# Expert stage of a decoder layer: the down product's two remainder matmuls, widened with zeros before, one in each row half of the array after

## The reference, cut to what matters

```
E, I, TOPK = 64, 192, 8
CAP = 2 * (M * TOPK) // E            # 256 token places per expert
...
h = silu(einsum('ecd,edi->eci', xe, gate_proj)) * einsum('ecd,edi->eci', xe, up_proj)
ye = einsum('eci,eid->ecd', h, down_proj)
out = zeros((m, d)).at[tok].add(contrib)   # contrib: the rows of ye, weighted
x = x + out
```

## Time and profile before

| | us |
|---|---|
| median of three runs | 1675.92 |
| lowest and highest of them | 1671.69 to 1676.97 |
| span of the profiled execution, first to last instruction | 1678.1 |
| expert stage in it, from the first transfer of its POOL program on | about 542 |

### The profile page before, as it was taken

How to read it: one execution, slowest core, us unless ns; L and a number is a source line. 1 busy time by engine, 2 the same in 40 slices (tenths; PEclk the granted TensorE clock), 3 DMA queues, 4 the chain that set the end, 5 groups by cost and what they waited for, 6 DMA issues and landing times. The chain is left out here.

```text
span 1678.1 us, 28691 instructions
## 1 busy us (share of the span) xinstructions
PE 1419.7 (85%) x9603; PEld 1053.1 (63%) x9603; DVE 1050.1 (63%) x2044; ACT 972.8 (58%) x1969; POOL 759.6 (45%) x492
## 2 busy tenths in 40 slices
PE   2889889899986767898898887856999999999990
PEld 2677777677764533444444433336999999999980
DVE  4666666667663533434443449855888888888880
ACT  3555455455552335674574575625777777777770
POOL 2344344444431013633533430003777777777762
PEclk9989999999997989998998998877999999999995
DMA  8000000000002276475466266055999999999986
GB/s 323 1 14 26 14 14 26 14 25 15 20 8 88 70 135 115 88 121 143 75 110 158 51 115 115 4 166 174 288 298 297 299 297 294 294 296 293 296 170 125
DMA packets 133106, 229.79 MB, mean 137 GB/s; under 512 B 17865, under 2 KB 51145, under 8 KB 132496
## 3 DMA queue, kind: packets, MB, share of 16 engines
q1 hardware_dynamic: 103184, 154.98, 34.0%
q0 software_dynamic: 29248, 72.53, 19.5%
q10 hardware_dynamic: 576, 0.98, 0.2%
HBM read 163.78 MB, written 71.83 MB: 140 GB/s over the span
## 5 line engine op out<-in xcount | busy, mean ns | idle before, releaser
L1045 ACT ACTIVATE shared<-xa_ring 128x1024 f32<-128x1024 f32 x256 | 247.0, 1030 | 94.1 <-PE xa_ring L1445 93.9
L1007 POOL TENSOR_TENSOR shared<-shared,xa_half 128x32 f32<-128x32 f32 x24 | 130.3, 5429 | 248.0 <-DVE shared L1168 248.0
L302 POOL TENSOR_TENSOR sa_prob<-sa_prob,sa_rinv 128x1024 f32<-128x1024 f32 x64 | 121.3, 1896 | 244.7 <-DVE sa_rinv L465 244.7
L1612 POOL DMA_INDIRECT ex_xg<-xn,token x128 | 173.9, 1359 | 82.2 <-issue 57.6
L360 ACT ACTIVATE sa_prob<-sa_sc_ps,sa_nmax 128x256 f32<-128x256 f32 x256 | 118.0, 473 | 111.1 <-DVE sa_nmax L452 111.1
L95 PE MATMUL ex_ba<-ex_xh,ex_wh 128*128 128x256 f32 x512 | 149.6, 292 | 4.4 <-DVE ex_xl L1726 3.7
L97 PE MATMUL ex_ba<-ex_xh,ex_wl 128*128 128x256 f32 x512 | 145.7, 285 | 0.0
L96 PE MATMUL ex_ba<-ex_xl,ex_wh 128*128 128x256 f32 x512 | 145.6, 284 | 0.0
L1457 PE MATMUL xa_out<-shared 128*17 128x512 f32 x1024 | 140.3, 621 | 0.5 <-ACT shared L1045 0.4
L1713 DVE TENSOR_TENSOR ex_wl<-shared,ex_wh 128x1024 fp32r<-128x1024 f32 (+1 forms) x128 | 116.9, 955 | 36.1 <-ACT ex_wh L1656 36.1
L452 DVE TENSOR_REDUCE sa_nmax<-sa_sc_ps 128x2 f32<-128x512 f32 x128 | 83.1, 687 | 66.5 <-PE sa_sc_ps L597 66.5
(11 more groups left out here) (223 smaller groups left out, 3939.7 us busy)
## 6 DMA issues: line engine op xcount, KB each, us to landing
shared<-in_L_ffn_gate_proj_dram SPq DMA_DIRECT2D x64, 384.0 KB, 5.7
shared<-in_L_ffn_up_proj_dram SPq DMA_DIRECT2D x64, 384.0 KB, 7.3
turned<-stage SPq DMA_DIRECT2D x64, 256.0 KB, 2.8
shared<-in_L_ffn_down_proj_dram SPq DMA_DIRECT2D x64, 256.0 KB, 5.0
xa_kT<-turned SPq DMA_DIRECT2D x96, 128.0 KB, 8.3
xa_qT<-turned SPq DMA_DIRECT2D x96, 128.0 KB, 10.5
shared<-in_L_ffn_down_proj_dram SPq DMA_DIRECT2D x64, 128.0 KB, 6.3
sa_x<-in_x_dram SPq DMA_DIRECT2D x16, 256.0 KB, 2.8
```

The costliest lines, as they stand in the source:

```text
L302: pool.tensor_tensor(prob[:, 4 * g:4 * g + 4, :], prob[:, 4 * g:4 * g + 4, :], rinv[:, 4 * g:4 * g + 4].unsqueeze(2).to_broadcast([P, 4, 2 ...
L1007: pool.tensor_tensor(power[:, i], ms[:, i], half[:], ALU.pow).then_inc(s_pw, 1)
L1045: act.activation(prob[:, w % 2, 2 * i:2 * i + 2, :], ring[i][:], ACT.Exp, scale=D2 ** -0.5).then_inc(s_ex[i], 1)
L1612: pool.indirect_dma_start(out=xg[:, e % RING, j, :], out_offset=None, in_=xn3, in_offset=bass.IndirectOffsetOnAxis(token[:, at:at + 1], 0))\
```

## The change

The low by high product of the remainder takes 64 rows of the array for each token tile in place of 128. Token tile 0 keeps its low part of h in rows 0 to 63 and is multiplied by `dh[0:64, i, 1]`; token tile 1 has its low part of h in rows 64 to 127 and is multiplied by a new tile `dr`, a copy of the same high part of the down matrix in rows 64 to 127. The two matmuls stand side by side at the end of `down`, after the four others of both token tiles. For that ACT makes one more copy for each expert, from partitions 0 to 63 to partitions 64 to 127; DVE makes `hl` of the remainder in two pieces of 128 columns in place of one of 256, the second one into partitions 64 to 127; and nothing is set to zero any more. PE and SP wait for the new copy.

```diff
--- before.py
+++ after.py
@@ -1535,6 +1535,7 @@
         wl = m.sb("wl", [P, 2, C, 3, P], F32R)
         dh = m.sb("dh", [P, 2, 2, D], F32R)
         dl = m.sb("dl", [P, 2, D], F32R)
+        dr = m.sb("dr", [P, 2, D], F32R)
         xg = m.sb("xg", [P, RING, CT, XW])
         xh = m.sb("xh", [P, 2, C, CAP], F32R)
         xl = m.sb("xl", [P, 2, C, CAP], F32R)
@@ -1550,7 +1551,7 @@
 
         ld_g = [m.sem(f"ld_g{k}") for k in range(RING)]
         st_y = [m.sem(f"st_y{k}") for k in range(RING)]
-        st_out, s_zero = m.sem("st_out"), m.sem("zero")
+        st_out = m.sem("st_out")
         counters = []
 
         def counter(name):
@@ -1597,6 +1598,7 @@
                     wait(sp, s_wl, 2 * e + 2)
                     weights_of.load_gate_up(sp, e + RING, k)
                     wait(sp, s_dl, DL * e + DL)
+                    wait(sp, s_dh, 3 * e + 3)
                     weights_of.load_down(sp, e + RING, k)
 
             loop(sp, lambda: None, step, lambda: None)
@@ -1625,7 +1627,6 @@
                                             oob_is_err=False, compute_op=ALU.add)\
                         .then_inc(st_y[e % RING], 16)
 
-            pool.memset(hl[R:2 * R, :, 1].bitcast(F32), 0.0).then_inc(s_zero, 1)
             gather(0)
             gather(1)
             for e in range(E):
@@ -1660,6 +1661,7 @@
                 wait(act, s_dn, 2 * e - 2)
                 act.activation(dh[:, i, 0], rawd[:, k, 0], ACT.Copy).then_inc(s_dh, 1)
                 act.activation(dh[0:R, i, 1], rawd[0:R, k, 1], ACT.Copy).then_inc(s_dh, 1)
+                act.activation(dr[R:2 * R, i], rawd[0:R, k, 1], ACT.Copy).then_inc(s_dh, 1)
 
             def tokens(e, i):
                 for j in range(CT):
@@ -1713,9 +1715,9 @@
                     dve.tensor_tensor(lo, src, hi.bitcast(F32), ALU.subtract).then_inc(s_wl, 1)
 
             def down_weights(e, i, k):
-                dve.wait_ge(s_dh, START + 2 * e + 1)
+                dve.wait_ge(s_dh, START + 3 * e + 1)
                 dve.tensor_tensor(dl[:, i], rawd[:, k, 0], dh[:, i, 0].bitcast(F32), ALU.subtract).then_inc(s_dl, 1)
-                dve.wait_ge(s_dh, START + 2 * e + 2)
+                dve.wait_ge(s_dh, START + 3 * e + 2)
                 dve.tensor_tensor(dh[R:2 * R, i, 1], rawd[0:R, k, 1], dh[0:R, i, 1].bitcast(F32),
                                   ALU.subtract).then_inc(s_dl, 1)
 
@@ -1733,7 +1735,10 @@
             def inner_low(e, i):
                 dve.wait_ge(s_hh, START + 3 * e + 2)
                 dve.tensor_tensor(hl[:, i, 0], h[:, i, 0], hh[:, i, 0].bitcast(F32), ALU.subtract).then_inc(s_hl, 1)
-                dve.tensor_tensor(hl[0:R, i, 1], h[0:R, i, 1], hh[0:R, i, 1].bitcast(F32), ALU.subtract).then_inc(s_hl, 1)
+                for j in range(CT):
+                    at = slice(j * P, (j + 1) * P)
+                    dve.tensor_tensor(hl[j * R:(j + 1) * R, i, 1, at], h[0:R, i, 1, at], hh[0:R, i, 1, at].bitcast(F32),
+                                      ALU.subtract).then_inc(s_hl, 1)
 
             def store(e, k, r):
                 dve.wait_ge(s_dn, START + 2 * e + 2)
@@ -1784,7 +1789,8 @@
             def down(e, i):
                 pe.wait_ge(s_dl, START + 2 * e + 2)
                 pe.wait_ge(s_hh, START + 3 * e + 3)
-                pe.wait_ge(s_hl, START + 2 * e + 2)
+                pe.wait_ge(s_hl, START + 3 * e + 3)
+                pe.wait_ge(s_dh, START + 3 * e + 3)
                 for j in range(CT):
                     wait(pe, (s_yA, s_yD)[j], e)
                     at = slice(j * P, (j + 1) * P)
@@ -1792,10 +1798,12 @@
                             lambda c: dl[:, i], 1, stop=False)
 
                     pe.matmul(by[j][:], hh[:, i, 1, at], dh[:, i, 1], start=False, stop=False)
-                    pe.matmul(by[j][:], hl[:, i, 1, at], dh[:, i, 1], start=False, stop=True).then_inc(s_dn, 1)
+
+                for j, rest in enumerate((dh[0:R, i, 1], dr[R:2 * R, i])):
+                    pe.matmul(by[j][:], hl[j * R:(j + 1) * R, i, 1, j * P:(j + 1) * P], rest, start=False,
+                              stop=True).then_inc(s_dn, 1)
 
             def first():
-                pe.wait_ge(s_zero, 1)
                 turn(0, 0, 0)
 
             def step(e, k, r):
```

## The result

The changed kernel takes 1698.99 us (median of 4 runs, 1696.4 to 1706.46) against 1673.81 us for the kernel before (median of 4, one run more than in the table above): 1.0154 times as long, 95% interval 1.0124 to 1.0185. That is some 25 us slower; forecast were 16, between 4.6 and 22.6, so the result lies above the range.

What follows compares the result with a forecast made beforehand. PE, waiting for `xl` in a loop through ACT and DVE, was taken as the bound. 61 x 0.29 = 17.7 us, less 1 for long experts and 0.5 at the start, gave +16 us: 1692 us, range 1680 to 1698.

Steps and rivals of the forecast that it cites:

- What bounds the kernel before: Per expert, a loop of `up` (PE), silu (ACT), h and `xl` (DVE) sets the period, 7.56 us; PE waits for `xl`.
- The copy on ACT: ACT's new copy `dr` ahead of the `wh` copies: 0.77 us against 0.48 slack, so h comes 0.29 us later per expert.
- The pair on PE: The two half matmuls ending `down`: 0.43 to 0.45 us with both switches, against 0.46 before; gains 0.01 to 0.03 us.
- The store on ACT now waits: Token tile 0's last matmul comes later in `down`, so ACT's store starts 0.26 us too late.
- the second loop: Store and copies on ACT, `wl` and h on DVE, `hh` copies, next store: 7.08 us, 7.85 with the new copy.
- The two-expert loop: From the late store through copies, `wl`, h, `xl`, `up` and down: 0.55 us longer, 0.27 to 0.28 per expert.
- The long experts: Experts that already took longer, 1.3 us in all, would mostly be taken in by a loop with slack on PE: -1 us.
- The two loops counted once: The second loop and the two-expert loop run side by side, so 0.29 us per expert was counted only once.
- DVE, POOL, the start: Split `hl` on DVE and POOL's work cost nothing; without zeros POOL's first gather starts earlier, -0.5 us or nothing.
- No change: Rival, about 1676 us: the loop over `up` stays the bound, the copy hides in ACT's 1.57 us wait; chance 0.10.
- faster: Rival, about 1661 us: PE is the bound, the pair takes one matmul's time, saving 0.23 us per expert; chance 0.04.
- slower still: Rival, above 1700 us: PE's switches cost say 0.3 us each, not 0.10, making the store 0.2 later; chance 0.06.

## Why the prediction was right in its direction and too small

**What bounds the kernel before.** Right. PE waits for `xl` by a hair: with the wait moved back the period fell to 7.48 us, 7.47 was expected of that run.

**The copy on ACT.** Right, in place and in size: 0.78 us for 0.77, a period of 7.86 for 7.85, and 0.53 for a copy that stays in its partitions, where 0.52 was put. The rows of L1678, a copy of another length, gave the price.

**The pair on PE.** Wrong. It was put at 0.43 to 0.45 us for 0.46, neutral. The switch in (0.32 for 0.33) was read rightly; the way back was taken from a switch to yet another small division, 0.33 us, and to the full array it is 0.42 to 0.43, with a first matmul of `up` that is 0.11 longer. The pair alone loses 0.16 us per expert. In the changed kernel the way back is hidden, since the other loops are longer: with the other order in `up` its period is 7.86 us, that of the copy, and not PE's 7.64.

**The store on ACT now waits.** Right as a mechanism, and here lies the missed size: "the same as the second loop within what I can read". The two-expert loop was put at 2 x 7.56 + 0.55 = 15.67 us and is 15.88 (7.85 + 8.03) or 16.12 (7.85 + 8.27). The step that failed is the size of one term, the way from the start of the pair to the store, put at 0.40 + 0.04 = 0.44 us ("ends 0.40 later", and ACT sees it 0.04 later). A half whose weights are not loaded ahead is listed with 0.50, and the earlier trace rows had it so. The store comes 0.53 us after the pair even in the written-out steps, and 0.64 in the hardware loop, with 0.11 of it for the scale's address, a term that the forecast did not have. That is 0.20 per two experts, 15.87 for the 15.88 measured, and 30 x 0.20 = 6 us.

**The long experts.** Wrong by sign: 1 us was taken off because a loop with slack on PE would take them in. The loop of the copy does, in the run with the copy alone. The two-expert loop runs through PE and does not: in the twelve long turns of it the loop takes 0.23 us more on average, 3 us in all. These and the 6 above are about what lies between 16 and 25.

**The two loops counted once.** Half right. The longer one counts, which is what was said; but it was the two-expert loop, at 7.99 us on average, and not 7.85. With 7.85 the sum gave 16 us, and the run with the copy alone, where only that loop is there, took 16.6 in its stage.

**DVE, POOL, the start.** The split `hl` costs no time: the run without the copy has it, and is PE's. From ACT's first copy of the stage (1135.55 before, 1127.01 after) to the first transposes it is 7.89 us in the one and 7.79 in the other, so leaving out the zeros gave back 0.1 us, not 0.5.

**The rivals.** No change and faster both needed a copy below 0.48 us, and fell with it; faster also needed a pair that PE does in less time than the two matmuls, and it took 0.16 us more. Of slower still, the mechanism was the right one, a later store, but from another cause than a dearer switch.

## What to carry to other kernels

Where several engines stand in loops of nearly one length, what counts is not whether an instruction fits into an engine's idle time but whether it stands ahead of something that another engine waits for: ACT waited some 1.6 us for `up` in each expert, and the copy of 0.78 us still made the period 0.27 us longer, because it stood ahead of the `wh` copies. Small matmuls in parts of the array paid for a switch in and a switch out here, and one pair in place of two of ten full matmuls lost 0.16 us. Several pairs in a row would share the two switches; in cross attention the second pair starts 0.33 us after the first, where two full matmuls take 0.46. No run of the experts tried that. And before a product is made shorter, it is worth asking what the next one really waits for: another order of the matmuls in `up` made the kernel 0.6% faster.

## What was not expected of the hardware

From the start of a pair of row halves to the next matmul of the full array are 0.42 us, and that one is listed 0.11 us longer; to another small division it was 0.33 us. In the hardware loop ACT's store, after its wait, starts 0.11 us later when the address of its scale depends on the expert. And on PE the first `up` of a turn of that loop starts 0.16 to 0.24 us late from the second turn on. The hold of ACT at a copy that changes partitions was expected; the two runs with the copy give its price, 0.25 us for one of 64 x 512.
